# Idle TensorE matmuls between the router logits and the coefficient transposes of three routing stages

## What is computed

```python
x = x + tanh(g_xattn[l]) * attention_l(layernorm(x), ctx, ...)
x = x + tanh(g_ffn[l])   * moe_l(layernorm(x), ...)
# layer 0: 8 low-rank adapters, the best 2 of the router's 8 outputs weigh them
# layer 1: 64 experts: sigmoid scores, the best 4 of 8 groups, then the best 8 experts
# layer 2: 14 experts, the best one
# layer 3: an attention of its own, then 8 experts, the best 2
```

## Time and profile before

| | us |
|---|---|
| median of 3 runs | 1325.06 |
| lowest and highest run | 1324.38, 1332.39 |
| the profiled execution, its own time | 1331.9 |
| span of the profile (first to last instruction) | 1329.6 |
| TensorE busy with matmuls in it | 994.4 (75%) |
| VectorE, ScalarE, GpSimd busy | 870.6, 671.4, 459.4 |
| mean granted TensorE clock | 0.861 |

### The profile page before, as it was taken

One profiled execution on the slowest core, in us unless ns is written; L12 is line 12 of the kernel. 1 busy time (PEld: TensorE's weight loads), 2 busy tenths in 40 slices (PEclk: granted clock), 3 DMA queues, 4 the chain that ended last, 5 costly groups with the idle time before them and its releaser, 6 DMA issues. The chain is left out here.

```text
span 1329.6 us, 29123 instructions
## 1 busy us (share of the span) xinstructions
PE 994.4 (75%) x10103; PEld 508.2 (38%) x10103; DVE 870.6 (65%) x1756; ACT 671.4 (50%) x1308; POOL 459.4 (35%) x575
## 2 busy tenths in 40 slices
PE   3578867888359999999757773290778777786997
PEld 2344544545324444444322243170444432233342
DVE  4568647887656677676668966153778669953453
ACT  2157512476235555555327850150267427873786
POOL 3105200453125555555403522405003202211786
PEclk7779958799579999999879995595889977995899
DMA  7731203210034444433261100311521051101332
GB/s 214 257 120 36 60 1 105 74 51 3 0 89 133 126 131 123 133 122 132 73 238 34 34 2 2 89 41 50 164 94 36 1 161 34 34 2 32 90 96 71
DMA packets 110782, 109.34 MB, mean 82 GB/s; under 512 B 16028, under 2 KB 86884, under 8 KB 109637
## 3 DMA queue, kind: packets, MB, share of 16 engines
q1 hardware_dynamic: 107350, 92.33, 23.1%
q10 hardware_dynamic: 2288, 13.31, 2.7%
q0 software_dynamic: 1024, 2.10, 0.5%
HBM read 83.83 MB, written 23.53 MB: 81 GB/s over the span
## 5 line engine op out<-in xcount | busy, mean ns | idle before, releaser
L758 ACT ACTIVATE work<-ps 128x384 f32<-128x384 f32 (+1 forms) x640 | 303.8, 533 | 166.5 <-PE ps L614 105.2
L857 DVE TENSOR_REDUCE bmax<-ps 128x6 f32<-128x768 f32 (+1 forms) x320 | 335.6, 1056 | 61.5 <-PE ps L592 44.6
L1612 POOL TENSOR_TENSOR work<-Ks,work 128x512 f16<-128x512 f32 x196 | 227.1, 1159 | 183.7 <-ACT work L1691 178.5
L1625 PE MATMUL ps<-ao,wf 128*128 128x512 f16 x984 | 248.1, 384 | 8.4 <-DVEq L1712 4.3
L1735 DVE TENSOR_TENSOR Ks<-ps,Qs 128x512 f32<-128x512 f32 x192 | 132.7, 692 | 57.8 <-ACT ps L1683 48.2
L603 PE MATMUL ps<-Qs,Ks 32*128 32x256 f16 x640 | 122.3, 291 | 56.7 <-issue 19.4
L1641 PE MATMUL ps<-work,wf 128*128 128x512 f16 x588 | 160.9, 383 | 2.5 <-POOL work L1612 2.5
L636 PE MATMUL ps<-work,V 128*9 128x256 f32 (+1 forms) x2560 | 155.1, 362 | 0.0
L895 POOL TENSOR_SCALAR mx<-bmax 128x16 f16<-128x16 f32 x80 | 25.1, 313 | 373.4 <-DVE bmax L863 219.1
L1625 PEld LDWEIGHTS ps<-ao,wf 128*128 (+1 forms) x984 | 88.4, 98 | 140.3 <-issue 44.3
L1683 ACT ACTIVATE work<-ps 128x512 f32<-128x512 f32 x132 | 78.8, 598 | 113.7 <-PE ps L1625 113.7
(11 more groups left out here) (233 smaller groups left out, 1547.6 us busy)
## 6 DMA issues: line engine op xcount, KB each, us to landing
Qs<-scrC SPq DMA_DIRECT2D x256, 128.0 KB, 3.0
Qs<-scrQ SPq DMA_DIRECT2D x40, 256.0 KB, 3.1
Ks<-scrK SPq DMA_DIRECT2D x40, 256.0 KB, 3.4
Qs<-scrC SPq DMA_DIRECT2D x32, 256.0 KB, 3.2
scrK<-work SPq DMA_DIRECT2D x60, 128.0 KB, 2.1
scrQ<-work SPq DMA_DIRECT2D x60, 128.0 KB, 2.6
Qs<-mxT SPq DMA_DIRECT2D x320, 1.0 KB
wf<-in_L_w ACTq DMA_DIRECT2D x2, 1792.0 KB, 9.6
```

The costliest lines, as they stand in the source:

```text
L758: act.activation(prob[:, g % 8, 0:W1], ps[:, 4 + g % 3, 0:W1], ACT.Exp, scale=float(att["dk"]) ** -0.5).then_inc(exped, 1)
L857: dve.tensor_reduce(bmax[:, n // 4 % 2, 2 * (n % 4):2 * (n % 4) + 2, 0:NB], ps[:, b0:b0 + 2, 0:W1].rearrange("p i (n w) -> p i n w", n=NB) ...
L1612: pool.tensor_tensor(hparts[:, (m + r) % 4, 1, :], weighted(m + r), hparts[:, (m + r) % 4, 0, :], ALU.subtract).then_inc(second, 1)
L1625: ins = pe.matmul(out, weight_parts(which, wpart, j), xh[:, xpart, c * CH:(c + 1) * CH], start=(i == 0), stop=(i == 2))
```

## The change

A new semaphore `s_chosen` is incremented by VectorE's group mask in layer 1. After the logits TensorE now waits for `s_chosen` (layer 1) or `s_d` (layers 0 and 3), issues 36 (layer 1) or 24 (layers 0 and 3) matmuls whose result nobody reads, into bank 3, and then waits for `s_c` as before. Each has 32 rows, 128 weight columns and 512 moving columns.

```diff
+    s_chosen = sem(f"r{l}_groups_chosen")
...
             ins.then_inc(s_l, 1)
+            if l == 1:
+                pe.wait_ge(s_chosen, 1)
+            else:
+                pe.wait_ge(s_d, 1)
+            for k in range(36 if l == 1 else 24):
+                pe.matmul(ps[:, 3, :], st["place"][0:32, 0, :], st["keep"][0:32, 0:CH], start=True, stop=True)
             pe.wait_ge(s_c, 1)
...
-                dve.tensor_tensor(gs, gs, wide(top[:, :, 3], G), ALU.is_ge)
+                dve.tensor_tensor(gs, gs, wide(top[:, :, 3], G), ALU.is_ge).then_inc(s_chosen, 1)
```

## The result

The changed kernel takes 1345.82 us (median of 4 runs, 1343.54 to 1352.22) against 1327.89 before (the three runs of the table and a fourth); the ratio is 1.0105, 95% interval 1.0053 to 1.0157. The ratio is not the quotient of the two medians, which is 1.0135 here; the two can differ by up to 0.003, and the text goes by the ratio and its interval. A second set, timed later beside 23 runs of the kernel before, gives 1346.05 against 1329.88 and 1.0128 (1.0094 to 1.0162), some 17 us. Both intervals lie above 1: it is slower, as forecast.

What follows compares the result with a forecast made beforehand. VectorE's chain bounds the gaps before the transposes, where TensorE waits; idle matmuls past that cover cost one for one. Delays 7.6 + 3.05 + 6.3 = 16.9 us on the 1325.06 median gave 1342 us, range 1326 to 1348.

Steps and rivals of the forecast that it cites:

- The sum: Delays of the first transposes: 7.6 us in route 0, 3.05 in route 1, 6.3 in route 3, together 16.9 us.
- The 0.427 us of one: Cost of one 512-column idle matmul at clock 0.50: 24 take 10.25 us, 36 take 15.4.
- VectorE's chain as the only cover: In the gaps before the transposes, VectorE's chain hides 2.7, 12.3 and 4.0 us of the streams in routes 0, 1, 3.
- The step on which all hung: In the three streams, 32-row matmuls leave the clock at 0.50, as four earlier windows show; low to the end, chance 0.50.
- The rival's price: Stream raises the clock 4.0 to 5.2 us in, so the time ends not slower: 1326.5 or 1322 us, chance 0.20.
- Part 4 of that page: Skill page says transposes don't raise the clock; the prediction objected that only route 1's transposes ran before the rise at 379.9.
- The shift loses expert stage 1 its clock: Delayed route 1 transposes make expert stage 1 start at the low clock, 3 to 6 us on top: 1346.5 us, chance 0.12.
- The part given back: Delays stay, but a stage behind the streams rises sooner, returning 3 to 6 us: 1337 us, chance 0.16.
- one of the prediction's own signs of being wrong: Stages behind the routes change by more than a few us; others: clock 1.00 within a stream, expert stage 3 keeping 1.00.
- 0.66 on slower by over 1%: Chance that the whole kernel's time lies above 1338.3 us, the upper edge of what a measurement can't tell from no change.

Runs made afterwards that it cites:

- fitted counts: The changed kernel with 6, 28 and 9 idle 32-row matmuls in routes 0, 1 and 3 instead of 24, 36 and 24: 1327.72 us, ratio 0.9975.
- doubled ones: The changed kernel with twice the idle 32-row matmuls, 48, 72 and 48 in routes 0, 1 and 3: 1381.75 us, ratio 1.0378 against before.
- route 1 alone: The changed kernel with its 36 idle 32-row matmuls in route 1 only, none in routes 0 and 3: 1333.84 us, ratio 1.0031 against before.
- 128 rows: The changed kernel with idle matmuls over all 128 rows instead of 32, same counts 24, 36, 24: 1332.31 us, ratio 1.0021 against before.
- 64 rows: The changed kernel with 64 rows instead of 32 in the idle matmuls, same counts 24, 36, 24: one run, 1343.33 us.
- bridges behind the transposes: Kernel before plus 4, 8, 8 full-row idle matmuls after the transposes of routes 0, 1, 3, during ScalarE's copies, no earlier streams: 1325.04 us, ratio 0.9968.
- full rows that fit: The changed kernel with 128-row idle matmuls, 6, 36 and 9 in routes 0, 1 and 3: 1328.3 us, ratio 1.0001 against before.
- bridges and streams: Kernel before plus early full-row streams (10, 42, 13) and 4, 8, 8 full-row idle matmuls after the transposes: 1324.26 us, ratio 0.994; repeated 1323.22, 0.9938.

## Why the prediction was right

**The sum.** 7.6 + 3.05 + 6.3 = 16.9 was forecast; 7.7 + 3.1 + 6.4 = 17.2 is in the profile, and some 17 in the medians. The 1342 itself was started from a median before of 1325.06, of three runs, where 23 runs put it at 1329.9; so 1345.8 is measured, 4 us above the forecast, though the difference is right. The 0.427 us of one, the moments of `s_d` and `s_chosen`, and VectorE's chain as the only cover held to a tenth. The fitted counts show that nothing else costs (ratio 0.9951 to 0.9999), the doubled ones that it costs one for one.

**The clock.** The step on which all hung was the reading of the earlier trace rows, that a 32-row stream leaves the clock low. It held in all nine streams of the change and its repeat and of the doubled kernel, up to 30.7 us long, and in the four of the fitted counts and of route 1 alone. The rival's price was about right for its own case: with 128 rows the rise comes 4.8 to 5.9 us into the stream (4.0 to 5.2 assumed), routes 0 and 3 are 5.5 and 3.6 us late (4.4 to 5.1 and 3.1 to 3.7), and the time is 2.4 us over before (+1.5 worked out). What it is about the rows is not shown: with more rows more products are formed as well, and no kernel here varied one without the other. By the Trainium skill, "TensorE: Matmul & The Clock Gate", Part 1, activity releases the throttle: the full-row streams agree, the 32-row and 64-row ones, as unbroken, do not, and the measurement decides. Part 4 of that page, which the prediction says the trace contradicts, speaks of TensorE's transpose mode; the views name the kernel's transposes MATMUL and show no mode, so the rows show that the clock rose behind these transposes with nothing else before them, and not more. That rise, at 379.9, also came 0.4 us behind the end of route 1's transposes (375.87 + 3.62 = 379.49) and not in them, as the prediction has it among the rivals.

**The rivals.** *The shift loses expert stage 1 its clock.* Its twelve first products began at the high clock in the profile of the change and of the doubled kernel (2.75 us), and low in the second profile of the change (4.30) and in those of route 1 alone (4.35), of 64 rows (4.13) and of the fitted counts (4.11). The last one has no delay, and its time is not over before. So low starts are real in single executions, but that the shift brings them is not shown; one profile of the kernel before can't say how often it has them. In the times the 3 to 6 us on top don't appear (4 us for route 1 alone, 17 for all, against 3.1 and 17.2), though the intervals leave room for some 4 of them.

*The part given back* (1337) is what the profiled execution looks like, with 5.5 us of luck, and it meets one of the prediction's own signs of being wrong, a stage behind the routes that changes by more than a few us. The kernel with a stream in route 1 only has the same early rise in expert stage 3, so the stream before it isn't the cause; and as a property of the kernel the second set of runs, 1.0094 to 1.0162, excludes 5 us of it. Less than that stays possible.

**Chances.** 0.66 on slower by over 1% was the right side, and it was near the bound: 17 us is 1.3%, and both intervals (from 1.0053 and from 1.0094) reach below 1.01.

## What to carry to other kernels

An idle matmul is free only until the work it waits beside has ended; count the cover in us (here 2.7, 12.3 and 4.0) and the stream at the low clock, since it starts there: 24 matmuls of 512 columns are 10.2 us, not 5.2. Look in the trace for a stretch made of the very instruction that is to warm TensorE, before it is used for that: here such stretches had left the clock at 0.50. And a raised clock is worth what the work behind it saves. Full-row streams before the transposes alone gave nothing clear (1.0001 and 0.998), no more than 32-row ones that fitted the cover (0.9975); bridges behind the transposes gave 0.3%, and with both it was 0.6%, twice. How much of that the streams add is open.

## What the runs showed of the hardware that was not expected

Neither 32 nor 64 rows raised the clock, in 30.7 and 15.4 us without a pause, while 128 rows of the same values raised it within 4.8 to 5.9 us. The 32-row and 64-row matmul takes as long as the full one, 0.427 us at the low level, so the smaller one saves no time.

The length of one pause doesn't tell whether a raised clock is kept. It fell behind pauses of TensorE of 2.2 us (194.4 to 196.6, all 128 rows), 2.9 us (372.1 to 375.0, full rows that fit; low from 376.0) and 3.05 us (up to 1222.5, bridges and streams). It stayed up over pauses of 2.0 and 2.6 us (377.5 to 379.5 and 381.4 to 384.0, all 128 rows) and of 3.1 us (1221.5 to 1224.6, bridges alone). Why it does the one or the other is not shown here.
